# The order of the attention's first tiles, of an ordinary pair's steps and of the tail, in an attention and feed-forward layer

## The reference

```python
c_kv = x @ w_dkv;  c_q = x @ w_dq                      # 64 and 192 columns
k = concat([rope(x @ w_kr) (one for all heads), (c_kv @ w_uk) per head])   # 64 + 128
q = concat([rope(c_q @ w_qr), c_q @ w_uq])             # 16 heads, 64 + 128
v = (c_kv @ w_uv) per head
attn = softmax(q k^T / sqrt(192))
x = layernorm(x + (attn v) @ w_o)
w1q, w3q, w2q = ternary(w1), ternary(w3), ternary(w2)  # -s, 0 or s
h1 = x @ w1q.T;  h3 = x @ w3q.T
x = layernorm(x + (silu(h1) * h3) @ w2q.T)
```

## Time and profile before

| What | Value |
| --- | --- |
| median of three timed executions | 929.67 us (928.97 to 929.88) |
| the profiled execution | 925.24 us |
| its span, from the first to the last instruction | 923.4 us |
| mean granted TensorE clock, as a share of full speed | 0.983 |
| PE busy | 869.9 us, 94% of the span |
| PEld busy | 499.6 us, 54% |
| DVE busy | 665.6 us, 72% |
| ACT busy | 692.4 us, 75% |
| POOL busy | 618.9 us, 67% |

### The profile page before, as it was taken

How to read it: one execution, slowest core, us unless ns; L and a number is a source line. 1 busy time by engine, 2 the same in 40 slices (tenths; PEclk the granted TensorE clock), 3 DMA queues, 4 the chain that set the end, 5 groups by cost and what they waited for, 6 DMA issues and landing times. The chain is left out here.

```text
span 923.4 us, 16915 instructions
## 1 busy us (share of the span) xinstructions
PE 869.9 (94%) x5128; PEld 499.6 (54%) x5128; DVE 665.6 (72%) x1055; ACT 692.4 (75%) x1113; POOL 618.9 (67%) x436
## 2 busy tenths in 40 slices
PE   8999689999999999989889969999999999998985
PEld 5668344444444444468666724444444444446874
DVE  2779678878788788844566957787878888783455
ACT  3744799999999999951353489999999999994142
POOL 0328777888788887851344766888888887885134
PEclk9899999999999999999999979999999999999998
DMA  9856799998998898980502679999899889898001
GB/s 253 251 197 139 154 205 189 177 183 161 176 190 165 159 194 170 171 193 31 200 23 55 140 153 197 188 173 183 161 175 186 166 160 197 168 168 213 5 1 46
DMA packets 423932, 145.82 MB, mean 158 GB/s; under 512 B 408188, under 2 KB 416208, under 8 KB 423120
## 3 DMA queue, kind: packets, MB, share of 16 engines
q1 hardware_dynamic: 423152, 142.91, 75.6%
q0 software_dynamic: 576, 2.10, 0.6%
q10 hardware_dynamic: 160, 0.26, 0.1%
HBM read 23.85 MB, written 7.60 MB: 34 GB/s over the span
## 5 line engine op out<-in xcount | busy, mean ns | idle before, releaser
L464 POOL TENSOR_TENSOR P_parts<-probs,P_parts 128x768 f16<-128x768 f32 x256 | 420.1, 1646 | 113.9 <-ACT P_parts L521 113.6
L521 ACT ACTIVATE P_parts<-probs 128x768 f16<-128x768 f32 x256 | 215.5, 842 | 11.0 <-DMA PT_dma<-P_parts 1.8
L896 DVE TENSOR_REDUCE small<-OO 128x1 f32<-128x1024 f32 x96 | 117.2, 1221 | 25.0 <-PE OO L1207 25.0
L1207 PE MATMUL OO<-K_hi,Q_parts 128*128 128x512 f16 x384 | 116.9, 386 | 16.9 <-DVE Q_parts L873 9.9
L1236 PE MATMUL Tb<-PT_dma,V_hi 128*64 128x512 f16 x768 | 132.3, 385 | 0.0
L906 DVE TENSOR_TENSOR PT_lo<-Ta,PT_hi 128x512 f16<-128x512 f32 x128 | 88.4, 690 | 59.9 <-ACT PT_hi L521 59.8
L896 DVE TENSOR_REDUCE small<-Sa 128x1 f32<-128x1024 f32 x96 | 116.9, 1218 | 19.0 <-PE Sa L1207 19.0
L628 ACT ACTIVATE probs<-OO,small,scales 128x1024 f32<-128x1024 f32 x96 | 115.1, 1199 | 10.3 <-DVE small L899 10.3
L1207 PE MATMUL Sa<-K_hi,Q_parts 128*128 128x512 f16 x384 | 117.3, 388 | 4.5 <-ACT probs L628 3.2
L628 ACT ACTIVATE probs<-Sa,small,scales 128x1024 f32<-128x1024 f32 x96 | 115.5, 1203 | 4.9 <-issue 3.8
L896 DVE TENSOR_REDUCE small<-Sb 128x1 f32<-128x1024 f32 x64 | 77.9, 1218 | 17.3 <-PE Sb L1207 17.3
(11 more groups left out here) (299 smaller groups left out, 1550.0 us busy)
## 6 DMA issues: line engine op xcount, KB each, us to landing
Q_parts<-turned_parts SPq DMA_DIRECT2D x64, 128.0 KB, 2.4
TT<-ternary SPq DMA_DIRECT2D x2, 2304.0 KB, 8.8
Q_parts<-Q_parts SPq DMA_DIRECT2D x16, 256.0 KB, 3.0
PT_dma<-P_parts SPq DMA_TRANSPOSE x256, 3.9
ternary<-tern SPq DMA_DIRECT2D x1, 2304.0 KB, 10.1
wo<-in_L_attn_w_o_dram SPq DMA_DIRECT2D x4, 512.0 KB, 8.4
xq<-in_L_attn_x_dram SPq DMA_DIRECT2D x2, 1024.0 KB, 13.4
wq_low<-Wq_lo SPq DMA_DIRECT2D x1, 2048.0 KB, 14.5
```

The costliest lines, as they stand in the source:

```text
L464: nc.gpsimd.tensor_tensor(P_parts[:, n % DEEP, 1, :], probs[n % DEEP][:, KP * P:S], P_parts[:, n % DEEP, 0, :], ALU.subtract).then_inc(par ...
L521: return nc.scalar.activation(o, i, ACT.Copy, scale=scale)
L896: nc.vector.tensor_reduce(nmax[:, n % 4:n % 4 + 1], scores_bank(n)[:, :], AX.X, ALU.max, negate=True).then_inc(row_max, 1)
L1207: last = mm(bank[:, m * HALF:(m + 1) * HALF], Q_parts[:, p * 2 + a, part, q:q + P], c[:, m * HALF:(m + 1) * HALF], start=(k == 0), stop=(k ...
```

## The change

- **Start of a batch's attention.** DVE takes tile 0's maximum directly behind the last `rotate`, ahead of the low parts of the last group of query terms. The two high copies of that group's rotary columns move from ACT to DVE (in the steps 0 and 2 of the first pair), the low parts on POOL and SP's moves one tile later. ACT gets one small exponential, `exp_warm`, behind the rotary copies of the third group.
- **Ordinary steps on PE.** Where `n` is not 0 or 8 and values stand in the step, PE takes the score tile `n+3`, the values (and the row of sums), the score tile `n+4`, then the transposes. Where `n` is 0 or 8, the order of before stays.
- **Ordinary steps on ACT.** In all pairs but the first and the last (of which only its first step) it takes the exponential of `n+2`, the casts of `n+1` and `n+2`, the exponential of `n+3`, then the copy of the transposes.
- **Tail.** The order on PE, DVE and ACT changes as the diff shows; `Y_BANKS` (the down products' PSUM banks) are other ones for six of the eight row tiles; the input's bound of the next batch uses another bank and comes earlier on ACT and PE; the second norm of the last four row tiles, its root and its store go in two pairs.
- **Weights.** SP's load of the low query weights for the second batch (2 MB) moves from the end of batch 0 to behind the loads of the next batch's input and tables.

```diff
-        Y_BANKS = (SQ[2], SQ[3], SQ[2], SQ[3], SQ[2], SQ[3], Ta[:, :], Tb[:, :])
+        Y_BANKS = (SQ[2], SQ[3], Ta[:, :], Tb[:, :]) * 2
...
+                    sp.wait_ge(att_ps, b * QT)
+                    sp.wait_ge(att_res, (b - 1) * 48 + 24)
+                    sp.dma_start(Wq_lo[:, :, :, :].rearrange("p h c m -> p (h c m)").bitcast(F), wq_low).then_inc(wq_in, 16)
...
-                        if first and n in (4, 6):
+                        if first and n in (5, 7):
...
-                if b + 1 < B:
-                    sp.wait_ge(att_ps, (b + 1) * QT)
-                    sp.wait_ge(att_res, b * 48 + 24)
-                    sp.dma_start(Wq_lo[:, :, :, :].rearrange("p h c m -> p (h c m)").bitcast(F), wq_low).then_inc(wq_in, 16)
...
-                        if first and n in (1, 3):
-                            rotary_parts_low(GROUPS - 1, n // 2)
+                        if first and n in (2, 4):
+                            rotary_parts_low(GROUPS - 1, n // 2 - 1)
...
+                def store(h, part=0):
+                    pool.wait_ge(y_ready, b * 3 + Y0 + (1 if h == 0 else part + 2))
+                    rows = slice(2 * part if h else 0, 2 * part + 2 if h else 4)
+                    nc.gpsimd.dma_start(out_v[b][:, 4 * h + rows.start:4 * h + rows.stop, :], yo[h][:, rows, :]).then_inc(y_out, 16)
...
+                power(slice(4, 6), 4)
+                power(slice(6, 8), 5)
+                store(1, 0)
+                store(1, 1)
...
+                    if g == GROUPS - 2:
+                        nc.scalar.activation(exp_warm, cq_up, ACT.Exp, scale=0.0)
...
+                    def cast(m):
+                        part_high(t0 + m, m, None if first and m < DEEP else 16 * (t0 // DEEP + m // DEEP))
...
                     for n in range(0, TILES, 2):
                         ahead = not (last and n == TILES - 2)
+                        before = not first and not (last and n > 0)
+                        behind = first and n < TILES - 2 or last
                         if ahead:
                             exponent(t0 + n + 2, n + 2)
-                            part_high(t0 + n + 2, n + 2, None if first and n + 2 < DEEP else 16 * (t0 // DEEP + (n + 2) // DEEP))
+                            if before:
+                                cast(n + 1)
+                            cast(n + 2)
                             exponent(t0 + n + 3, n + 3)
                         transposed_high(t0 + n + 1, n + 1)
-                        if ahead:
-                            part_high(t0 + n + 3, n + 3, None if first and n + 3 < DEEP else 16 * (t0 // DEEP + (n + 3) // DEEP))
-                        if first and n == 0:
-                            rotary_parts_high(GROUPS - 1, 1)
+                        if ahead and behind:
+                            cast(n + 3)
...
-                rotary_parts_high(GROUPS - 1, 0)
...
-                for t in range(HT):
+                silu(0, 0)
+                silu(0, 1)
+                gate_high(0, 0)
+                gate_high(0, 1)
...
                     silu(0, t)
                     gate_high(0, t)
-                    if t == 3:
+                    if t == 4:
                         x1_high(1)
                 silu(1, 0)
                 silu(1, 1)
+                if b + 1 < B:
+                    squares(b + 1)
                 gate_high(1, 0)
                 gate_high(1, 1)
-                if b + 1 < B:
-                    squares(b + 1)
                 for t in range(2, HT):
                     silu(1, t)
                     gate_high(1, t)
...
-                for g in range(GROUPS):
-                    rotate(g)
-                    latents_low(g, 0)
-                    if g:
-                        rotary_parts_low(g - 1)
-                    if g < GROUPS - 1:
-                        latents_low(g, 1)
...
+                for g in range(GROUPS):
+                    rotate(g)
+                    if g == GROUPS - 1:
+                        maximum(b * PAIRS * TILES, 0)
+                    latents_low(g, 0)
+                    if g:
+                        rotary_parts_low(g - 1)
+                    latents_low(g, 1)
+
+                def rotary_parts_high(g, j):
+                    dve.wait_ge(rope_sum, b * 2 * GROUPS + 2 * g + j + 1)
+                    dve.wait_ge(turned_out[j], b * 64 * GROUPS + 64 * g)
+                    nc.vector.tensor_copy(turned_parts[:, j, 0, :], turned[:, j, :]).then_inc(rope_hi, 1)
...
+                        if first and n in (0, 2):
+                            rotary_parts_high(GROUPS - 1, n // 2)
...
-                maximum(b * PAIRS * TILES, 0)
-                latents_low(GROUPS - 1, 1)
...
-                attention_rows(1)
+                for t in range(4, 7):
+                    attention_row(t)
                 gate_tile(0, 0)
-                first_norm(1)
+                attention_row(7)
+                add_eps(slice(4, 8), A0 + 24)
                 gate_tile(0, 1)
                 gate_tile(0, 2)
+                first_norm(1)
                 gate_tile(0, 3)
+                gate_tile(0, 4)
                 x1_low(1)
-                for t in range(4, HT):
+                for t in range(5, HT):
                     gate_tile(0, t)
                 gate_tile(1, 0)
                 gate_tile(1, 1)
-                result_rows_0()
+                result_rows_0(0)
                 if b + 1 < B:
                     input_norm(b + 1)
+                result_rows_0(2)
+                add_eps(slice(0, 4), A0 + 36)
...
-                second_norm(0)
+                second_norm(range(4), 3)
...
-                result_rows_1()
+                result_pair(4, A0 + 36)
+                result_pair(6, A0 + 42)
                 dve.sem_inc(y_read, 1)
-                second_norm(1)
+                second_norm(range(4, 6), 4)
+                second_norm(range(6, 8), 5)
...
                     pe.wait_ge(x_max, batch + 1)
-                    nc.tensor.transpose((Sa, Ta)[batch][0:1, 0:P], x_most, ident[:, :]).then_inc(x_row, 1)
+                    if batch:
+                        pe.wait_ge(att_res, (batch - 1) * 48 + 25)
+                    nc.tensor.transpose((Sa, SQ[2])[batch][0:1, 0:P], x_most, ident[:, :]).then_inc(x_row, 1)
...
-                        next_scores(n + 3)
-                        if n % 8 != 4:
-                            next_scores(n + 4)
-                        for i in range(2):
-                            transpose_probs(t0 + n + i, pair * (TILES // 2) + n // 2, n + i, ahead)
-                        if n % 8 == 4:
-                            next_scores(n + 4)
-                        if first and n == 8:
-                            pe.wait_ge(v_in, b * 32 + 32)
-                        if not (first and n < 8):
-                            if n % 8 == 2:
-                                pe.wait_ge(exp_done, EXP0 + t0 + n + 3)
-                                sums_to_rows(pair * 2 + n // 8 - 1, ROW_BANK)
+                        valued = not (first and n < 8)
+
+                        def next_values():
                             for k in range(n % 8, n % 8 + 2):
                                 values(pair * 2 + n // 8 - 1, 1 - n // 8, k)
+
+                        def next_transposes():
+                            for i in range(2):
+                                transpose_probs(t0 + n + i, pair * (TILES // 2) + n // 2, n + i, ahead)
...
+                        next_scores(n + 3)
+                        if n % 8 == 0:
+                            next_scores(n + 4)
+                            next_transposes()
+                            if first and n == 8:
+                                pe.wait_ge(v_in, b * 32 + 32)
+                            if valued:
+                                next_values()
+                        else:
+                            if valued:
+                                next_values()
+                                if n % 8 == 2:
+                                    pe.wait_ge(exp_done, EXP0 + t0 + n + 3)
+                                    sums_to_rows(pair * 2 + n // 8 - 1, ROW_BANK)
+                                next_scores(n + 4)
+                                next_transposes()
+                            else:
+                                if n % 8 != 4:
+                                    next_scores(n + 4)
+                                next_transposes()
+                                if n % 8 == 4:
+                                    next_scores(n + 4)
...
-                            if i == 0 and u < 6:
-
-                                pe.wait_ge(att_res, b * 48 + (24 if u < 2 else 24 + 3 * (u - 2) + 1))
+                            if i == 0 and u < 2:
+                                pe.wait_ge(att_res, b * 48 + 24)
+                            elif i == 0 and u >= 4:
+                                pe.wait_ge(att_res, b * 48 + 24 + 3 * (u - 4) + 1)
...
```

(15 more changed lines are left out.)

79 lines of the change are left out of this document (37 added, 42 removed).

## The result

The changed kernel took 920.12 us in the median (917.82 to 921.86, four runs), the kernel before 929.32 (928.38 to 929.88, four runs): ratio 0.990, interval 0.9875 to 0.9926. It is faster, as forecast, but by 9.2 us instead of 19.6.

A forecast was written before the change was run, and what follows sets the result against it. PE was taken to bound the attention loop, ACT 0.85 behind. Starts -4.1 and -5.8, loop -2.2, prefetches +2.0, last pairs -3.0, tails -3.8 and -1.7, end -1.0 sum to -19.6: from 929.67 to 910 us, range 900 to 924.

The forecast's parts named there:

- The start: Start of each batch's attention: earlier maximum, table load and copies gain 4.1 us in batch 0, 5.8 in batch 1.
- rival 3: Start gives little: POOL held 1.3 by each of four DVE copies, or PE at half clock; 917 us, chance 0.13.
- The prefetches: Eight output-weight prefetches: SP issues two more DMAs ahead of the even tile's; 0.25 each, 2.0 us lost, between 0 and 8.
- The loop: Attention halves: tile 8's wait goes, tile 7 waits 0.12, half 18.80; 28 halves gain 2.2 us.
- the rule: Attention loop: the score tile behind the transposes waits for ACT's exponential of two tiles before; 0.12 at tile 7.
- rival 2: Each change of kind on PE costs like a values entry; loop loses 6.2 instead of winning 2.2: 918 us, chance 0.15.
- Rival 4: Ring of cast tiles: back-to-back DMAs land too late, each half waits; 938 us with 1.0 of wait, chance 0.10.
- Last pairs: End of a batch's last pair: values block moved inside the last transposes' wait; 1.5 per batch, 3.0 us gained.
- Tails: Behind each batch's attention: fewer PE waits around residual rows, hidden and down products; 3.8 us gained in batch 0, 1.7 in batch 1.
- end: Very end: two rows instead of four between last product and last store; 1.0 us gained, between 0 and 2.

The follow-up runs named there:

- Twice the moves: Changed kernel with each of the last query group's two sets of rotary moves issued twice by SP in the first pair: 935.96 us.
- SP alone edited: Changed kernel with the last query group's landing wait and rotary moves earlier in SP's queue: 916.76 us, ratio 0.9895 to the kernel before.
- the part taken off POOL: Changed kernel with SP's earlier moves, plus one of POOL's two low parts of the last rotary group done by DVE: 918.01 us.
- the run without that edit: Changed kernel with PE's old order (except a batch's last step), casts in twos through the last pair, SP's moves earlier, prefetches between tiles 0 and 1: 904.5 us.

## Why the prediction was wrong, step by step

**The start: the step that failed.** The prediction ended its sum for the start at the engines' first tiles and put the queue behind them at nothing: what waits behind SP's moves "waited about as long before: 0". The engine times themselves came out. In the changed kernel (PE, ACT):

```profile
534.40 0.61 PE L1232 MATMUL OO<-K_hi,Q_parts 128*128 128x512 f16 x2 [2.21 <-DVE Q_parts L886]
...
563.64 0.64 PE L1261 MATMUL Tb<-PT_dma,V_hi 128*64 128x512 f16 x2 [2.79 <-DMA PT_dma<-P_parts]
```

```profile
528.72 1.28 ACT L648 ACT_TABLE_LOAD   x1
537.84 1.19 ACT L631 ACTIVATE probs<-OO,small,scales 128x1024 f32<-128x1024 f32 x1
563.59 0.84 ACT L524 ACTIVATE P_parts<-probs 128x768 f16<-128x768 f32 x1 [2.06 <-DMA PT_dma<-P_parts]
```

The table load stands at 528.72, off the path; the third score tile waits 2.21 in place of 5.70, and comes 3.48 earlier, forecast 3.2; the third exponential 4.42 earlier than in the earlier trace rows, forecast 4.0; tile 8's exponential 6.2 earlier behind tile 0's scores, forecast 5.8. In batch 0 tile 4's exponential came 4.7 earlier, forecast 4.1. But by tile 16 only 2.06 and 0.79 of that was left. SP in batch 1, before and then after:

```profile
540.89 9.75 SPq L363 DMA_TRANSPOSE PT_dma<-P_parts  x4
550.69 2.85 SPq L333 DMA_DIRECT2D Q_parts<-turned_parts  x4
553.66 3.36 SPq L363 DMA_TRANSPOSE PT_dma<-P_parts  x2
557.07 2.79 SPq L333 DMA_DIRECT2D Q_parts<-turned_parts  x4
559.97 20.34 SPq L363 DMA_TRANSPOSE PT_dma<-P_parts  x10
```

```profile
540.03 9.76 SPq L367 DMA_TRANSPOSE PT_dma<-P_parts  x5
549.83 2.80 SPq L337 DMA_DIRECT2D Q_parts<-turned_parts  x4
552.75 3.31 SPq L367 DMA_TRANSPOSE PT_dma<-P_parts  x2
556.11 3.01 SPq L337 DMA_DIRECT2D Q_parts<-turned_parts  x4
559.24 19.03 SPq L367 DMA_TRANSPOSE PT_dma<-P_parts  x9
```

In both, SP takes the first transposing DMA at 540 to 541, since it waits for the landing of the group's moves, and issues eight moves, some 2.8 for four, between the DMAs of the first tiles. So tile 7's DMA, about 561.6 before (the second of the ten), left at 559.24, 2.3 earlier, although its exponential came 5.54 earlier and POOL was done with it at 555.2. Its landing ended the 2.79 of PE and the 2.06 of ACT in the fences above. Before, no wait over 0.3 of PE or ACT in batch 1's first pair was ended by such a DMA, and in batch 0's only one, of 1.26. What the engines gained in front, they now stood in line for at this queue. In batch 0 the wait came at tile 4's cast, for tile 0's DMA, which SP took at 108.64 behind the same landing:

```profile
110.53 1.20 ACT L631 ACTIVATE probs<-Sb,small,scales 128x1024 f32<-128x1024 f32 x1
114.13 0.84 ACT L524 ACTIVATE P_parts<-probs 128x768 f16<-128x768 f32 x1 [2.30 <-DMA PT_dma<-P_parts]
```

At tile 16 0.8 and 2.1 were left of the 9.9, so seven were lost. Of these, 2.5 is the price of the new orders in the first pair, which the prediction lacked: with the start undone, tile 16 comes 1.60 and 0.86 later than in the kernel before. The other 4.6 was lost by the start itself. Twice the moves show that SP's queue has no time to spare here, and SP alone edited won back 1.34 and 0.85 by tile 32. That the queue took all of the 4.6 isn't shown; no run takes the moves out of it without a price elsewhere. What rival 3 named instead was small: the part taken off POOL changed nothing, and from tile 0's scores to tile 16's exponential the mean granted clock was 0.89 in batch 1 (before 0.86) and 0.96 in batch 0 (before 0.96).

**The prefetches: the right place, the wrong size.** They were put at 0.25 each, bounded by 1; in a gap of the queue the three of each loop cost 2.5 less, 0.85 each. SP, then the cast and the score tile that waited (batch 0):

```profile
185.59 0.70 SPq L373 DMA_DIRECT2D Wvo_lo<-wvo_low  x1
186.34 0.43 SPq L375 DMA_DIRECT2D xr<-in_L_attn_x_dram  x1
187.23 14.17 SPq L367 DMA_TRANSPOSE PT_dma<-P_parts  x7
```

```profile
191.79 0.84 ACT L524 ACTIVATE P_parts<-probs 128x768 f16<-128x768 f32 x1 [0.74 <-DMA PT_dma<-P_parts]
```

```profile
193.96 0.60 PE L1232 MATMUL OO<-K_hi,Q_parts 128*128 128x512 f16 x2 [0.97 <-ACT probs L631]
```

From 185.59 to 187.23 the two issues hold SP, 1.64, between tile 15's and tile 0's DMAs, which the casts in twos now bring back to back; between tile 0's and tile 1's there is a gap.

**The loop: the rule held, the credit was given to the wrong edit.** The forecast half was 18.80 with a wait of 0.12 at tile 7; the trace has 18.81 to 18.91, and there it is, 0.56 behind transposes for 0.44, with scores ahead of values at 1.40 each. Yet the 2.2 forecast did not come: with the prefetches in the gap a loop takes 188.65, and 188.66 before. Tile 7 in the changed kernel:

```profile
640.73 0.61 PE L1232 MATMUL OO<-K_hi,Q_parts 128*128 128x512 f16 x2
642.13 0.41 PE L1261 MATMUL Tb<-PT_dma,V_hi 128*64 128x512 f16 x2
645.34 0.60 PE L1243 MATMUL Ta<-ident,probs 128*128 128x128 f32 x4
645.90 0.60 PE L1232 MATMUL OO<-K_hi,Q_parts 128*128 128x512 f16 x2
```

PE without waits is 18.70 in the new order (18.82 less the 0.12) and 18.63 in the old, 0.07 for its additional entries, so rival 2 (0.30 a half) was nearly absent. But the wait of tile 8, which the new PE order was to remove, goes with the casts alone, at 18.63. I had taken ACT's new order for a cost that PE's new order pays for; it is the reverse. Rival 4, the ring of casts, came true in the loops only behind prefetches.

**The rest.** Last pairs gave 1.6 of 3.0. The values ahead of the last transposes were worth a little more than the 1.5 forecast: from tile 127's exponential to the first hidden tile 34.16 became 32.31 and 32.54, 1.85 and 1.62 less. But the score tiles ahead of it took 0.94 longer (18.82 became 19.46 up to tile 120, 16.28 became 16.58 from there), a term that the prediction lacked. With the casts in twos to the end and PE's old order they take 18.63 and 16.90.

Tails (-3.94 and -1.72, forecast -3.8 and -1.7) and end (-1.27, forecast -1.0) came out. The waits listed for the tails are there: batch 1's were put at 0.5, 0.9 and 0.8, and the trace has 0.44 (for DVE's x1b), 0.67 (for its x1T_lo) and 0.87 (for POOL's g_lo).

The exact match of the tails is in part luck: PE's standing fell by 3.25 and 1.17, less than the 3.8 and 1.7, and the other 0.69 and 0.55 came from PE being busy for less, which was not in the sum. Rival 3 was too dear, see below.

## What to carry to other kernels

Work that comes earlier is worth what the next resource in line can take earlier: follow a gain to the point where it is spent, through the queue that issues DMAs too, since the page shows no busy time for it. Where two orders are changed together, work out each with the other left old. And compare stretches cut at the same work, not spans, where a stretch ahead of the change wanders by 5 us; how far an unedited stretch differs from kernel to kernel says what a difference is worth.

## What the runs showed of the hardware

Rival 3 had POOL stand still for 1.3 per copy on DVE. The two copies of 1024 columns on DVE in batch 0 of the changed kernel, and two of POOL's subtractions:

```profile
108.31 0.68 DVE L918 CAST turned_parts<-turned 128x1024 f16<-128x1024 f32 x1
113.31 1.41 DVE L918 CAST turned_parts<-turned 128x1024 f16<-128x1024 f32 x1
```

```profile
108.42 2.07 POOL L464 TENSOR_TENSOR P_parts<-probs,P_parts 128x768 f16<-128x768 f32 x1 [0.42 <-ACT P_parts L524]
112.53 1.64 POOL L464 TENSOR_TENSOR P_parts<-probs,P_parts 128x768 f16<-128x768 f32 x1
```

The first copy began while POOL stood still and took 0.68; the subtraction that began 0.11 later took 2.07 instead of the 1.64 of the two beside it. The second copy began inside the subtraction from 112.53, which had 0.86 left, and took 1.41. So here the one that begins later loses, by 0.43 and 0.73, which is less than what was left of the other (0.57 and 0.86), and not 1.3 for POOL each time.

Issued by ACT, the eight moves landed 5.7 behind their issue in the median in batch 0 and 5.5 in batch 1; the same eight issued by SP, in the run without that edit, 2.7 and 2.5. And the issue of one transposing DMA took SP 1.54 in the median (24 of them in 526 to 600) of the 2.36 that a tile has in a half of 18.9, that of four plain moves 2.8 to 3.0. An estimate from these: over eight tiles the queue has 8 x 0.82 = 6.6 free, and eight moves take 5.8 of it.
